# First pair of a fused graph-convolution kernel: token and channel mixing ahead of the query and key weight products, the wait for x moved, the batch-norm folding in gaps

## The reference, cut to what matters

```python
# layer 0: node mixing, channel mixing, four branches, residual
x  = concat([x[:, :16], einsum('bctv,vw->bctw', x[:, 16:], A_flat)])
x  = concat([einsum(x[:, :16], A_intra), einsum(x[:, 16:], A_inter)])
d  = maximum(abs(A_learned).sum(1), 1e-6) ** -0.5
An = d[:, None] * abs(A_learned) * d[None, :]
y  = relu(bn(einsum('oc,bctv->botv', Wgc, x + einsum(x, An)), bn_gc))
b1, b2 = bn(tconv(relu(bn(c1x1(y, Wb))), Wt, dilation))      # one per branch
b3 = bn(max_over_time(relu(bn(c1x1(y, Wb3))))); b4 = bn(c1x1(y, Wb4))
t  = relu(concat([b1, b2, b3, b4]) + res)                    # res is x itself
# layer 1: attention over tokens, per group of images
Q = (n @ rot) @ Wq.T; K = (n @ ent) @ Wk.T; V = n @ Wv.T     # n = layer norm of t
t = t + softmax(exp(-|Q - K|^2)) @ V
# layer 2: batch norm of a projection, then a sigmoid recurrence over time
out = t + scan(sigmoid(wx_t + y @ V.T))
```

## Time and profile before

| | us |
|---|---|
| median of 3 runs | 230.27 (228.68 to 230.61) |
| profiled execution | 229.49 |
| its span, first to last instruction | 227.7 |
| PE busy | 196.7 (86%) |
| ACT busy | 169.7 (75%) |
| DVE busy | 161.2 (71%) |
| POOL busy | 28.7 (13%) |

### The profile page before, as it was taken

How to read it: one execution, slowest core, us unless ns; L and a number is a source line. 1 busy time by engine, 2 the same in 40 slices (tenths; PEclk the granted TensorE clock), 3 DMA queues, 4 the chain that set the end, 5 groups by cost and what they waited for, 6 DMA issues and landing times. The chain is left out here.

```text
span 227.7 us, 3379 instructions
## 1 busy us (share of the span) xinstructions
PE 196.7 (86%) x1150; PEld 96.0 (42%) x1150; DVE 161.2 (71%) x294; ACT 169.7 (75%) x307; POOL 28.7 (13%) x44
## 2 busy tenths in 40 slices
PE   0686999999999797979699999999999998599960
PEld 0562646545555443413234343434343423266640
DVE  0327819999999763894958497877777795576980
ACT  4028299789779698996988999999999974365640
POOL 6000000091060053080101010101010000000000
PEclk9997999999999999979999999999999999889995
DMA  6940020089799349199631607080800000000016
GB/s 188 370 135 3 3 72 1 1 227 296 194 259 340 100 146 304 42 353 252 173 79 40 179 10 212 0 219 0 219 3 0 3 0 0 0 3 3 0 50 241
DMA packets 26885, 26.87 MB, mean 118 GB/s; under 512 B 1550, under 2 KB 25806, under 8 KB 26740
## 3 DMA queue, kind: packets, MB, share of 16 engines
q1 hardware_dynamic: 26868, 26.64, 39.9%
HBM read 14.74 MB, written 11.88 MB: 117 GB/s over the span
## 5 line engine op out<-in xcount | busy, mean ns | idle before, releaser
L510 ACT ACTIVATE arena<-ps 128x800 f32<-128x800 f32 (+1 forms) x56 | 44.5, 797 | 6.9 <-PE ps L1053 4.6
L517 ACT ACTIVATE arena<-arena 128x800 f32<-128x800 f32 (+1 forms) x56 | 46.4, 831 | 0.0
L1053 PE MATMUL ps<-qa,ka 128*128 128x400 bf16 (+1 forms) x128 | 35.4, 340 | 3.6 <-ACT arena L510 2.0
L1053 PE MATMUL ps<-qb,kb 96*128 96x400 bf16 (+1 forms) x128 | 35.4, 339 | 0.0
L742 DVE TENSOR_TENSOR psum<-arena 128x400 f32<-128x400 f32 x32 | 19.6, 612 | 13.8 <-ACT arena L517 13.8
L742 DVE TENSOR_TENSOR psum<-psum,arena 128x400 f32<-128x400 f32 x32 | 19.5, 610 | 7.5 <-ACT arena L517 6.2
L1053 PEld LDWEIGHTS ps<-qa,ka 128*128 128x128 bf16 (+1 forms) x128 | 10.4, 97 | 27.6 <-ACT arena L510 12.5
L1086 PE MATMUL ps<-arena,vb 128*32 128x400 f32 x192 | 21.6, 525 | 0.2 <-issue 0.2
L751 DVE RECIPROCAL arena<-ps 128x400 f32<-128x400 f32 x7 | 18.6, 2650 | 0.0
L664 DVE COPY arena<-arena 32x400 f32<-32x400 f32 x48 | 17.2, 358 | 0.9
L587 ACT ACTIVATE yb<-ps 128x160 f32<-128x160 f32 x36 | 11.0, 305 | 8.0 <-PE ps L1170 6.7
(11 more groups left out here) (146 smaller groups left out, 354.3 us busy)
## 6 DMA issues: line engine op xcount, KB each, us to landing
dka<-arena SPq DMA_DIRECT2D x16, 200.0 KB, 3.1
dqa<-arena SPq DMA_DIRECT2D x16, 200.0 KB, 3.2
ka<-dka SPq DMA_DIRECT2D x8, 400.0 KB
qa<-dqa SPq DMA_DIRECT2D x8, 400.0 KB
arena<-x_tok SPq DMA_DIRECT2D x4, 400.0 KB
t<-x SPq DMA_DIRECT2D x1, 1600.0 KB, 11.7
dkb<-arena SPq DMA_DIRECT2D x8, 200.0 KB, 3.5
dqb<-arena SPq DMA_DIRECT2D x8, 200.0 KB, 3.7
```

Source lines behind the costliest of these rows:

```text
L510: nc.scalar.activation(prob[par][:, lo:hi, :], ps[:, o:o + hi - lo, 0:N], ACT.Exp, scale=2.0).then_inc(e1_done, 1)
L517: nc.scalar.activation(p, p, ACT.Exp).then_inc(p_ready, 1)
L1053: last = mm_(ps[row:row + keys, bank, 0:N], kk[par][0:rows, b, o:o + keys], qq[par][0:rows, b, :], start=first, stop=not first, skip_group ...
```

## The change

The two weight products for query and key are issued on TensorE after `mix_v(0)` and `mix_c(0)`, next to the product for `wc`. The wait for `late_in` stands before `mix_c(0)`, and the wait for `prep_done` before `taps(0)`. On VectorE three of the six batch-norm operations stand before the forming of `ia` and three behind it; a new semaphore `bn_ready` tells ScalarE that they are done. The copies to `aq` stand behind `y_copy(0)`. The wait for `x_in` stands before `add_x(0)`. Nothing is computed differently, and the DMA issues keep their order.

```diff
@@ ScalarE
-            act.wait_ge(prep_done, 1)
+            act.wait_ge(bn_ready, 1)
@@ VectorE, preparation
             link(nc.vector.tensor_scalar(dd, c_("ident", MT)[:, 0:MT], dcol, None, ALU.mult))
+            link(nc.vector.tensor_tensor(bn_s, bn_r, c_("bn_g"), ALU.mult))
+            link(nc.vector.tensor_tensor(bn_ms, bn_s, c_("bn_m"), ALU.mult))
+            link(nc.vector.tensor_tensor(bn_h, c_("bn_b"), bn_ms, ALU.subtract))
             dve.wait_ge(pe_c, 1)
             link(nc.vector.scalar_tensor_tensor(out=ia, in0=ps[0:MT, 2, 0:MT], scalar=dcol,
                                                 in1=c_("ident", MT)[:, 0:MT], op0=ALU.mult, op1=ALU.add))
+            link(nc.vector.tensor_tensor(bn_h2, bn_h, c_("keep"), ALU.mult))
+            link(nc.vector.tensor_tensor(bn_s, bn_s, c_("keep"), ALU.mult))
+            link(nc.vector.tensor_tensor(bn_s2, bn_s, c_("pass"), ALU.add))
+            dve.sem_inc(bn_ready, 1)
             dve.wait_ge(pe_c, 3)
...
             nc.vector.tensor_copy(mlo[:, 1, :], ps[0:MT, 0, 0:MT]).then_inc(mlo_ready, 1)
-            link(nc.vector.tensor_tensor(bn_s, bn_r, c_("bn_g"), ALU.mult))
-            link(nc.vector.tensor_tensor(bn_ms, bn_s, c_("bn_m"), ALU.mult))
-            link(nc.vector.tensor_tensor(bn_h, c_("bn_b"), bn_ms, ALU.subtract))
-
-            link(nc.vector.tensor_tensor(bn_h2, bn_h, c_("keep"), ALU.mult))
-            link(nc.vector.tensor_tensor(bn_s, bn_s, c_("keep"), ALU.mult))
-            link(nc.vector.tensor_tensor(bn_s2, bn_s, c_("pass"), ALU.add))
-            dve.wait_ge(pe_c, 6)
-            nc.vector.tensor_copy(aq[:, 0, :], ps[:, 6, 0:P])
-            nc.vector.tensor_copy(aq[:, 1, :], ps[:, 7, 0:P]).then_inc(prep_done, 1)
             dve.wait_ge(zeroed, 4)
@@ VectorE, first pair
-            dve.wait_ge(x_in, 16)
             y_copy(0)
+            dve.wait_ge(pe_c, 6)
+            nc.vector.tensor_copy(aq[:, 0, :], ps[:, 6, 0:P])
+            nc.vector.tensor_copy(aq[:, 1, :], ps[:, 7, 0:P]).then_inc(prep_done, 1)
             tap_inputs(0)
             dve.wait_ge(wc_done, 1)
             nc.vector.tensor_copy(wc[:, :], ps[:, 5, 0:P]).then_inc(wc_ready, 1)
+            dve.wait_ge(x_in, 16)
             add_x(0)
@@ TensorE
-            pe.wait_ge(dve_c, 3)
+            pe.wait_ge(dve_c, 6)
             mm_(ps[0:MT, 2, 0:MT], c_("intraT", MT), ia, start=True, stop=True).then_inc(pe_c, 1)
             mm_(ps[0:MT, 3, 0:MT], c_("interT", MT), ia, start=True, stop=True).then_inc(pe_c, 1)
-            pe.wait_ge(dve_c, 4)
+            pe.wait_ge(dve_c, 10)
             mm_(ps[0:MT, 0, 0:MT], c_("flatT", MT), t2, start=True, stop=True).then_inc(pe_c, 1)
-            pe.wait_ge(late_in, 16)
-            mm_(ps[:, 6, 0:P], c_("rotT"), c_("wqT"), start=True, stop=True).then_inc(pe_c, 1)
-            mm_(ps[:, 7, 0:P], c_("entT"), c_("wkT"), start=True, stop=True).then_inc(pe_c, 1)
             pe.wait_ge(mlo_ready, 1)
...
             mix_v(0)
-            pe.wait_ge(prep_done, 1)
+            pe.wait_ge(late_in, 16)
             mix_c(0)
+            mm_(ps[:, 6, 0:P], c_("rotT"), c_("wqT"), start=True, stop=True).then_inc(pe_c, 1)
+            mm_(ps[:, 7, 0:P], c_("entT"), c_("wkT"), start=True, stop=True).then_inc(pe_c, 1)
             mm_(ps[:, 5, 0:P], c_("center"), c_("wT"), start=True, stop=True).then_inc(wc_done, 1)
             branches(0)
+            pe.wait_ge(prep_done, 1)
             taps(0)
```

More of the change, by code:

```diff
@@ L177, in build @@
         operands_in = [sem("operands_in0"), sem("operands_in1")]
-        zeroed, abs_done, dve_c, act_c, pe_c, mlo_ready, prep_done = (
-            sem(n) for n in ("zeroed", "abs_done", "dve_c", "act_c", "pe_c", "mlo_ready", "prep_done"))
+        zeroed, abs_done, dve_c, act_c, pe_c, mlo_ready, prep_done, bn_ready = (
+            sem(n) for n in ("zeroed", "abs_done", "dve_c", "act_c", "pe_c", "mlo_ready", "prep_done", "bn_ready"))
         (v_mixed, y0_ready, mixed, y_ready, branched, zp_ready, mx_ready, u_ready, u_act, pooled, tapped, ts_ready,
```

## The result

| | before | changed |
|---|---|---|
| median, us | 230.67 (20 runs) | 229.5 (20 runs) |
| lowest run, us | 228.68 | 227.10 |
| ratio of the runs compared, 95% interval | | 0.9928 (0.9901 to 0.9955) |
| profiled execution, us | 229.49 | 227.46 |
| its span, us | 227.7 | 225.7 |

The medians are over all executions, while the ratio leaves out the ones that fell in a slower state (up to 236.19 us before), so it is not the quotient of the medians.

A forecast was written before the change was run, and what follows sets the result against it. The start was taken as one chain, with node mixing behind late constants and its first copy waiting for x. Branches 0.84 us earlier, other terms near 0, gave 229.76 - 0.84 = 228.9 us; main case 228.3 to 229.4, chance 0.57.

The forecast's parts named there:

- The folding costs nothing: Batch-norm operations on DVE: three fit each idle stretch (0.57 us into 0.83 and 1.15 us); cost 0, gain 0.
- The products leave the path: Query and key products no longer precede node mixing, which starts at 9.53 instead of 10.92, a shift of 1.39 us.
- x leaves the path: First `y_copy` starts at 11.05 instead of 13.87; the wait for x before `add_x` is hidden.
- Channel mixing on PE's list, partly at 1.2 GHz: Channel mixing starts at 12.39, 2.2 us earlier; with the clock rising at 14.0 it is done at 14.54.
- Three products before the branches: Three products after channel mixing take 1.0 us; branches start at 15.5 instead of 16.34, bounds 15.2 to 15.7 by clock.
- Taps: Taps shift with the branches, some 0.1 us of change if the clock drop near 20 us keeps its time.
- The sum: 0.84 us gained at the branches, taken off the mean of four times, 229.76, giving 228.9 us.
- A: Rival: all of x's wait at the first copy comes back, 2.8 us, time 227.0; chance 0.10.
- B: Rival: nothing moves, as tokens are missing at 9.53 or moved products and low clock eat the gain; 229.6; chance 0.20.
- C: Rival: slower, channel mixing and three products at 1.2 GHz; 230.9, or 232.9 if second group's taps too; chance 0.13.
- D: Rival: first copy waited on all of node mixing, not x; 0.4 us gained, 229.3; inside the main case.
- The shift is passed on: An early start carries in full from 26.08 us on, later pairs still 17.69 us apart.

The follow-up runs named there:

- the gaps filled: Changed kernel plus products of a zeroed tile in three later long idle stretches of TensorE (before taps, second group's attention and recurrence): ratio 0.9897, median 227.56 us.
- the two fills: Changed kernel plus zeroed-tile products in TensorE's early preparation waits: nine and one per gap (first run 0.9812), or eleven and two per gap (0.9785).
- the first experiment: Kernel before with only the wait for x moved, from the first copy of node mixing to the first residual addition: ratio 0.9898, median 228.11 us.
- thin fill: Changed kernel plus nine zeroed-tile products ahead of TensorE's first product and one in each of three preparation gaps: ratio 0.9812, again 0.9856.
- dense one: Changed kernel plus eleven zeroed-tile products ahead of TensorE's first product and two in each of three preparation gaps: ratio 0.9785, median 225.39 us.

## Why the prediction was right, and where its size was off

**The folding costs nothing.** Right: both gaps stayed open, the last copy of the mixing matrices ended 4.00 us behind the start of `dd` (before 4.07, folding back 4.08), and undoing it changed nothing that could be measured.

**The products leave the path.** Right that node mixing follows 0.06 us behind its matrices. The sum then took most of it back further down, for the low clock and for the two products themselves. What the prediction did not ask is what the wait for x would give alone: the runs show no gain from the reorder next to that (0.9898 and 0.9949 without it, 0.9928 and 0.9936 with it).

**x leaves the path.** Right, and shown from both sides: this wait alone gives 0.5 to 1.0% of gain, and putting it back turns the change into a loss of 0.6%.

**Channel mixing on PE's list, partly at 1.2 GHz.** Right in mechanism. The rise was taken between 13.5 and 14.59. In the profiled execution of the changed kernel it came near 14.4, worked out from the 2.23 us between 12.67 and 14.90 for four passes of 0.67 us at the low or half of that at the high level. In the changed kernel's second profile and in that with the folding back, channel mixing took 3.04 us and the first of the three products still stands 0.33 and 0.35 us from the next instead of 0.22, so the rise came behind 15.10 and 15.62. Their branches started at 15.88 and 16.42, outside the 15.2 to 15.7 set by the clock and inside only the widest bound, 16.8. That the rise keeps its time when the work moves was an assumption, and it held in one of these three. Two further kernels have the same order up to there: channel mixing took 2.10 us with the gaps filled and 3.04 with the products behind the branches.

**Three products before the branches.** This term was mis-sized: 1.0 us in the sum, 0.67 measured. The 0.33 was read from 16.01 to 16.34, where the next instruction is a branch product that needs the first `y_relu` (from 15.60, about 0.65 us), so it held part of a wait; back to back they stand 0.22 to 0.23 apart at the high level.

**Taps.** This term was put at nothing, some 0.1 us, on the condition that the clock drop near 20 us stays, and its vanishing was named as a sign of being wrong. It vanished in the profiled execution, in the second profile and in the one with the folding back: from the first taps to node mixing of the second pair they take 5.55, 5.56 and 5.56 us, before 5.92. The price given for that case, up to half a microsecond and then VectorE's copies as the bound, fits the 0.37 us and the 0.98 us wait for VectorE. The drop is there in both profiles with only the wait moved (6.11 and 6.20 us), in the one with x's wait back (5.90), and in the two fills whose node mixing ran at the high level. What sets it is open.

**The sum.** Predicted 0.84 us at the branches, to be passed on as it is. Counted from `dd`, the branches came 1.12, 0.40 and 0.31 us earlier in the three profiles of this order (changed, changed again, folding back), a mean of 0.61. At pair 1, also from `dd`, they gained 1.49, 0.78 and 0.68 us, a mean of 0.98; the difference of 0.37 is the drop that did not come. So the forecast is near the profiles by two errors that offset each other, a slow stretch that was longer in two of the three and a drop that was absent in all, and that is luck. The kernel before has one profile, so its side rests on one execution. The measured 1.7 us (1.0 to 2.3) is more than that mean; its lower end is near it. The profiles do not show where the rest would come from. The mean granted clock in the executions behind the ratio of 0.9936 was 0.976 for the changed kernel and 0.971 before, and no run separates what that gives from the shift, so I leave it open.

The absolute forecast, 228.9 us, was taken from four times with a mean of 229.76; the twenty have a median of 230.67, and from there the same gain leads to 229.8 (measured 229.5). Two workings were slightly off and changed nothing: with the rise at 13.5 or 14.59 channel mixing ends at 14.3 or 14.8, not 14.2 or 14.7, and with the rise 1.39 us earlier the branches come near 14.8 and the time is 228.3, not 15.1 and 228.5.

**The rivals.** A (all of x's wait arrives, 2.8 us) did not come: the first copy moved by 2.34 us, the branches by 0.77. B's condition is refuted: mixing started at 9.4 to 9.9 in the profiles with the reorder, and at 8.72 with the fill, so the tokens were there; its other road, products and low clock eating the gain, took part of it in two of the three profiles (0.78 and 0.68 us left at pair 1) and not all. C did not decide, but its mechanism is real: with x's wait put back, the forward move let channel mixing and three products run at 1.2 GHz and cost time, and a rise behind 16.06 was seen in the second profile of the thin fill. D fell with the first experiment.

**The shift is passed on.** Right: from the second pair's node mixing (pair 1 in the table) to pair 3's it is 35.39 us before and 35.40 after.

## What to carry to other kernels

When two conditions come true within 0.03 us of each other, the releaser that a profile names may be the harmless one: ask of each instruction what it needs and when each of these was there. Price a move in TensorE's list at the clock of the place to which the work is moved; work that comes earlier into a slow start may gain nothing. When two edits are made together, measure each alone: here moving one wait did as well as the whole change. An idle TensorE ahead of a chain of short dependent products can be worth filling, and then densely: a thin fill brought about 225 us in four of twelve runs and 226.7 to 229.1 in the others, a dense one 224.6 to 226.2 in all six.

## What the runs showed of the hardware

The windows print a granted clock of 1.00 at the start also where TensorE runs at 1.2 GHz: before the first change of level nothing is on record. The durations tell it, 2.85 to 2.94 us against 1.59 for the same 32 passes.

The level once gained can be lost again in the thin stretch of the preparation: with only x moved and the thin fill, the window from 6 to 9 us has a mean clock of 0.82 with TensorE busy 2.12 of 3 us, and the next has 0.50. How busy TensorE was in that window does not decide alone: with the same fill in the changed kernel it was busy 2.12 us there too, and the level held:

```profile
6.00:9.00 3.00, 2.12 (x17) 1.02 (x18) 1.77 (x9) 0.00 (x0) 0.00 (x0) 1.00 0.95 350
```

The late constants landed between 8.95 and 9.95 us in the profiles, all of kernels that issue the same loads in the same order (1.65 us plus 7.3 to 8.3), so whether TensorE waits for them depends on the execution.
